# Attention in a fused attention and feed-forward layer on eight cores: the value matmuls six chunks behind the scores, and one eviction for two score chunks

## The reference

```python
q, k, v = xn @ Wq.T, xn @ Wk.T, xn @ Wv.T          # 16 heads of 128; 4 heads for k and v
q, k = rope(rms_norm(q)), rope(rms_norm(k))
bias = einsum('bhsr,bhtr->bhst', Rq, Rk)            # rank 32, heads 0..11
bias[:, :4] = (bias[:, :4] + transpose(bias[:, :4])) * 0.5   # heads 0..3 symmetric
scores = q @ k.T / sqrt(128) + bias * graph_scale   # heads 12..15: no bias
scores = where(causal, scores, min)
out = softmax(scores) @ v
s = out @ Wo.T
```

## Time and profile before

| | us |
|---|---|
| three runs, median | 4767.55 |
| lowest, highest | 4765.06, 4774.42 |
| the profiled execution's own time | 4769.61 |
| its span on core 1, the slowest | 4767.8 |
| spans of the eight cores | 4740.7 to 4767.8 |

### The profile page before, as it was taken

The page is one execution under the profiler, slowest core; times in us unless marked ns, Lnnn a source line. Parts: engine busy times, 40 slices in busy tenths (PEclk is TensorE's granted clock), DMA queues, the critical chain, the costliest instruction groups (busy, mean ns, idle before and its releaser), DMA issues. The chain is left out here.

```text
span 4767.8 us, 39041 instructions; the slowest of 8 cores (4740.7 to 4767.8 us)
## 1 busy us (share of the span) xinstructions
PE 3630.5 (76%) x15274; PEld 1513.7 (32%) x15274; DVE 1171.4 (25%) x1403; ACT 876.4 (18%) x862; POOL 315.5 (7%) x311
## 2 busy tenths in 40 slices
PE   2676576766999998988999998846666767775974
PEld 1222122222444443433444443311222222221433
DVE  7132133333000000000000000024444454453006
ACT  2121022221000000001000000013333343442112
POOL 0000000000111110001111100000000000000000
PEclk9977777777999999999999999967787888997986
DMA  3202411122788774557788754540000000003448
GB/s 133 53 9 22 106 29 27 29 31 31 73 78 77 74 71 71 75 75 79 74 78 78 74 66 77 76 117 21 18 18 16 16 7 15 15 6 84 39 98 279
DMA packets 547238, 287.88 MB, mean 60 GB/s; under 512 B 457075, under 2 KB 528756, under 8 KB 540020
## 3 DMA queue, kind: packets, MB, share of 16 engines
q0 software_dynamic: 498480, 162.55, 32.6%
q1 hardware_dynamic: 48580, 122.82, 7.6%
HBM read 397.53 MB, written 50.33 MB: 94 GB/s over the span
## 5 line engine op out<-in xcount | busy, mean ns | idle before, releaser
L856 PE MATMUL p_dps<-p_hfm,p_dwb 128*128 128x512 bf16 x2816 | 630.5, 387 | 87.5 <-ACT p_gout L874 59.0
L784 PE MATMUL p_gps<-xn_fm,p_gwb 128*128 128x512 bf16 x2816 | 627.0, 381 | 35.5 <-DMA p_uwb<-wu 35.4
L791 PE MATMUL p_ups<-xn_fm,p_uwb 128*128 128x512 bf16 x2816 | 622.1, 379 | 0.0
L1235 ACT ACTIVATE p_ptb<-p_scr,st_bnegb 128x1024 bf16<-128x1024 f32 x320 | 366.7, 1148 | 633.2 <-DVE p_scr L1202 448.4
L817 DVE SCALAR_TENSOR_TENSOR p_hfm<-p_ups,c_ups,p_sg 128x1024 bf16<-128x1024 f32 x88 | 112.9, 1283 | 1502.8 <-ACT p_sg L806 1502.8
L856 PEld LDWEIGHTS p_dps<-p_hfm,p_dwb 128*128 128x128 bf16 x2816 | 278.4, 99 | 439.6 <-issue 124.6
L1111 PE MATMUL p_sc<-p_qg,p_kfm 128*128 128x512 bf16 x640 | 281.6, 454 | 165.3 <-DVE p_ogs L1178 97.3
L784 PEld LDWEIGHTS p_gps<-xn_fm,p_gwb 128*128 128x128 bf16 x2816 | 276.2, 98 | 373.1 <-issue 45.9
L791 PEld LDWEIGHTS p_ups<-xn_fm,p_uwb 128*128 128x128 bf16 x2816 | 275.6, 98 | 332.2
L806 ACT ACTIVATE p_sg<-p_gps,c_gates 128x1024 f32<-128x1024 f32 x88 | 98.0, 1114 | 1090.9 <-PE p_ups L791 1090.8
L670 PE MATMUL p_qps<-xn_fm,p_wbuf 128*128 128x512 bf16 x1024 | 265.0, 424 | 39.3 <-DMA p_wbuf<-wq 39.3
(11 more groups left out here) (135 smaller groups left out, 2344.4 us busy)
## 6 DMA issues: line engine op xcount, KB each, us to landing
p_gwb<-wg POOLq DMA_DIRECT2D x88, 512.0 KB, 8.9
p_uwb<-wu POOLq DMA_DIRECT2D x88, 512.0 KB, 10.7
p_dwb<-wd POOLq DMA_DIRECT2D x88, 512.0 KB, 5.7
p_xt<-x SPq DMA_DIRECT2D x32, 1024.0 KB, 7.0
y<-p_outb SPq DMA_DIRECT2D x16, 1024.0 KB, 10.6
p_wbuf<-wq POOLq DMA_DIRECT2D x16, 512.0 KB, 6.5
sp_q<-p_qout SPq DMA_DIRECT2D x64, 128.0 KB, 1.8
sp_g<-p_gout SPq DMA_DIRECT2D x32, 256.0 KB, 2.6
```

The lines of the kernel that those rows point to most:

```text
L784: tensor.matmul(gps[:, po + q4 * 512:po + (q4 + 1) * 512], gw_[:, ec * 128:(ec + 1) * 128], xn_cols(ec, hh * 1024 + q4 * 512, 512), start= ...
L791: mm = tensor.matmul(ups[:, po + q4 * 512:po + (q4 + 1) * 512], uw_[:, ec * 128:(ec + 1) * 128], xn_cols(ec, hh * 1024 + q4 * 512, 512), s ...
L856: mm = tensor.matmul(dps[:, oc4 * 1024 + q4 * 512: oc4 * 1024 + (q4 + 1) * 512], wv_[:, oc4 * 128:(oc4 + 1) * 128], hfm[:, ic * 1024 + q4 ...
L1235: scalar.activation(ptb[:, j0 * 512:(j0 + 2) * 512], scr[:, (pr % 3) * 1024:(pr % 3) * 1024 + 1024], AF.Exp, bias=bneg_b[:, col:col + 1]). ...
```

## The change

TensorE's stream in attention has the value matmul of chunk j - 6 instead of j - 3 behind the scores of chunk j; six of them, not three, stand at the head's end. VectorE evicts a pair whose two chunks both are unmasked by one copy of 1024 columns, after a wait for both; pairs with a masked chunk are evicted as before, in two parts. Buffers, their number, the semaphores' counts and ScalarE's stream stay the same.

```diff
@@ -1129,15 +1129,15 @@
                                     last.then_inc(eC.h, 1)
                                     eC.inc()
                                     ich += 1
-                                    if j >= 3:
-                                        jj = j - 3
+                                    if j >= 6:
+                                        jj = j - 6
                                         tensor.wait_ge(eEx.h, base_eEx + pbase + jj // 2 + 1)
                                         tensor.matmul(
                                             o_ps[:, (h % 2) * 512:(h % 2) * 512 + 512],
                                             vsb[:, jj * 512 + kv * 128: jj * 512 + (kv + 1) * 128],
                                             ptb[:, jj * 512:(jj + 1) * 512],
                                             start=(jj == 0), stop=False)
-                                for jj in range(max(0, nch - 3), nch):
+                                for jj in range(max(0, nch - 6), nch):
                                     tensor.wait_ge(eEx.h, base_eEx + pbase + jj // 2 + 1)
                                     tensor.matmul(
                                         o_ps[:, (h % 2) * 512:(h % 2) * 512 + 512],
@@ -1186,25 +1186,36 @@
                             for h in range(NH):
                                 if h >= 1:
                                     sums_evac(vector, h - 1)
-                                for j in range(nch):
+                                for j in range(0, nch, 2):
                                     pr = ich // 2
-                                    if pr >= 3 and ich % 2 == 0:
+                                    if pr >= 3:
                                         vector.wait_ge(eEx.h, base_eEx + pr - 2)
-                                    vector.wait_ge(eC.h, base_eC + ich + 1)
-                                    po = (pr % 2) * 1024 + (ich % 2) * 512
-                                    so = (pr % 3) * 1024 + (ich % 2) * 512
-                                    if j >= 4 * g:
-                                        k = j - 4 * g
-                                        op = vector.tensor_tensor(
-                                            scr[:, so:so + 512], sc_ps[:, po:po + 512],
-                                            masks[:, k * 512:(k + 1) * 512], ALU.add)
-                                    else:
-                                        op = vector.tensor_copy(
-                                            scr[:, so:so + 512], sc_ps[:, po:po + 512])
-                                    if ich % 2 == 1:
-                                        op.then_inc(eEv.h, 1)
+                                    po = (pr % 2) * 1024
+                                    so = (pr % 3) * 1024
+                                    if j + 1 < 4 * g:
+                                        vector.wait_ge(eC.h, base_eC + ich + 2)
+                                        vector.tensor_copy(
+                                            scr[:, so:so + 1024], sc_ps[:, po:po + 1024]
+                                        ).then_inc(eEv.h, 1)
                                         eEv.inc()
-                                    ich += 1
+                                        ich += 2
+                                        continue
+                                    for jc in (j, j + 1):
+                                        vector.wait_ge(eC.h, base_eC + ich + 1)
+                                        poc = po + (ich % 2) * 512
+                                        soc = so + (ich % 2) * 512
+                                        if jc >= 4 * g:
+                                            k = jc - 4 * g
+                                            op = vector.tensor_tensor(
+                                                scr[:, soc:soc + 512], sc_ps[:, poc:poc + 512],
+                                                masks[:, k * 512:(k + 1) * 512], ALU.add)
+                                        else:
+                                            op = vector.tensor_copy(
+                                                scr[:, soc:soc + 512], sc_ps[:, poc:poc + 512])
+                                        if ich % 2 == 1:
+                                            op.then_inc(eEv.h, 1)
+                                            eEv.inc()
+                                        ich += 1
                                 if h >= 1:
                                     tail(vector, h - 1)
                             sums_evac(vector, NH - 1)
```

## The result

The changed kernel takes 4674.4 us in the median of its executions and the kernel before 4771.7. In some executions of either kernel the cores of one die run at a lower granted clock and the time is longer (5109 and 4819 us for two of the changed kernel's); these medians count them, the ratios here leave them out. The ratio is 0.9805 (0.9782 to 0.9827), 93 us. Run again on another occasion it had 0.9769 (0.9735 to 0.9802). The forecast was 78 us, 4690.

The account below looks back on a forecast made before the run. The prediction took attention to be bound by a circle through ScalarE's exponential. Savings of 14.9, 39.4 and 23.5 us gave 78, so 4767.55 - 78 = 4690; the forecast's own range was 4676 to 4704 (0.65), the overall range 4658 to 4722.

Parts of the forecast that it names:

- What bounds the kernel: Attention, g = 1 to 3: no engine full; a chain bounds it, with 126.0 us of TensorE idle awaiting exponentials at L1135.
- the old circle: Attention at lag three: exponential, value matmul, second chunk's scores, eviction, next-but-one exponential; 3.64 us per two pairs, heads 4 to 11.
- What is late next: Attention after the change, per pair: TensorE's slots 1.72 (heads 0-3), score buffers 1.41 (4-11) and 1.20 (12-15).
- the buffer circle: Two PSUM score buffers: scores of pair p+2 wait for pair p's eviction; 2.82 us per two pairs in heads 4-11.
- The rival of a larger gain: VectorE releases TensorE in 0.14, circles 1.355 and 1.14: 85 us, 99 with edges; range 4655 to 4676, chance 0.12.
- The edges: Head entries and ends: 0.37 to 0.53 us against, other effects for; 0.3 a head either way, 14 us, taken as nothing.
- Heads 4 to 11: Attention, two score matmuls a chunk: 1.82 to 1.41 us a pair, 0.41 saved, 39.4 us in all.
- Heads 0 to 3: Attention, three score matmuls a chunk: 2.03 to 1.72 us a pair, 0.31 saved, 14.9 us in all.
- Heads 12 to 15: Attention, one score matmul a chunk: 1.69 to 1.20 us a pair, 0.49 saved, 23.5 us in all.
- the second rival: Larger gain in attention through a quicker VectorE release, 4668; with a copy of 0.69, 12 us more, 4656; chance 0.12.
- the third rival: Attention slower if TensorE stays longer at 1.2 GHz: granted clock 0.75 costs 115 us, 4805; chance 0.03.
- The clock as a way to slower: Attention, g = 1 to 3: a mean granted clock of about 0.79 would eat the 78 us; chance 0.03.

Follow-up runs that it names:

- e1: Kernel before with the value matmul's lag raised from 3 to 6 and 512-wide copies kept (changed kernel without the wide copy): ratio 0.9717, attention 1010.2 us.
- e2: Kernel before with the wide copy alone, the lag staying at three: ratio 1.0102, attention 1193.0 us.
- e5: Lag six, narrow copies, and TensorE's wait at a head's start moved to before its first value matmul; against the kernel before: ratio 0.9629, attention 974.8 us.
- e8: Kernel before plus nine needless matmuls ahead of TensorE's wait at each head's start (heads 2 to 15): ratio 0.9938, attention 1111.4 us.
- e7: Changed kernel plus nine needless matmuls ahead of TensorE's wait at each head's start; against the kernel before: ratio 0.9731, attention 1016.8 us.

## Why the prediction was right, and where its sizes were off

- **What bounds the kernel** was right: the wait of L1135 for the exponential went, and with it 99 us of attention time in g = 1 to 3, nothing in g = 0. e1 shows that the lag does all of it, and e2 that the wide copy alone makes the old circle 0.54 longer.
- **What is late next** was right for heads 4 to 11: the two score buffers. The way back from VectorE to TensorE was the term that was mis-sized: 0.25 taken, 0.15 measured, the buffer circle 2.71 and not 2.82. Over 96 and 48 pairs at 0.055 it is 8 us. I had the choice between this value and the 0.14 of ScalarE's way, and took the row of the same pair of engines. That row was of the wait for a product at a head's start. TensorE had been idle for 2 us there, but that isn't the reason: in e5 33 waits for an eviction end more than 1.5 us of idle time, and the way is 0.15 in all of them. Why the product's way is longer stays open. The rival of a larger gain, with 1.355 a pair, describes what happened, and the time (4674) lies in its range, 2 us under the forecast's own.
- **The edges** were the other mis-sized term. The step that failed is "I allow 0.3 either way and take nothing". It is seen best between e8 and e7, where the fill holds the clock up in both kernels and the change gains 104 us in heads 0 to 15. By the forecast's own sum, with the shorter way back, the rates give 85: 15, 45 and 26 in heads 0 to 3, 4 to 11 and 12 to 15, against 24.8, 49.2 and 30.0 measured. The other 19 us are 0.39 a head. In heads 0 to 3 the excess over the rate is 3.1, 3.3 and 3.5 us in g = 1, 2 and 3, the same however many pairs a head has, so it does lie at the edges. ScalarE in a head of g = 3, number 0 to 3, of e8 and of e7:

```profile
4027.20 2.44 ACT L1242 ACTIVATE p_ptb<-p_scr,st_bnegb 128x1024 bf16<-128x1024 f32 x2 [8.35 <-DVE p_scr L1209]
4031.28 1.15 ACT L1242 ACTIVATE p_ptb<-p_scr,st_bnegb 128x1024 bf16<-128x1024 f32 x1 [1.63 <-DVE p_scr L1209]
...
3999.95 2.44 ACT L1253 ACTIVATE p_ptb<-p_scr,st_bnegb 128x1024 bf16<-128x1024 f32 x2 [8.89 <-DVE p_scr L1204]
4002.89 1.15 ACT L1253 ACTIVATE p_ptb<-p_scr,st_bnegb 128x1024 bf16<-128x1024 f32 x1 [0.49 <-DVE p_scr L1204]
```

From the first exponential to the third it is 4.08 us in e8 and 2.94 in e7. That is 1.14 less, where the rate gives 0.31. The other 0.83 a head, 3.3 us in four heads, is the old kernel's stand at the first exponential, which the forecast named among the edges and took as nothing.

- **Heads 4 to 11** of the pair itself: 39.4 us forecast, 37.4 measured on core 1 (470.7 to 433.3). This is partly luck of the core: by the medians of the eight cores it is 44. On core 1 a worse clock in g = 1 hides some of the gain: heads 4 to 7 had run at 1.00 before and have 0.91 now, and gained only 1 us where 3 were due.
- **Heads 0 to 3**: 14.9 forecast, 26.8 measured (263.1 to 236.3); 26.5 by the medians. It is the edges above, and no matter of the clock, since it is 24.8 with the fill.
- **Heads 12 to 15**: 23.5 forecast, 35.5 measured (230.1 to 194.6); 33 by the medians. A part of the excess is the clock's, and my sentence that the clock's part was in the 0.3 a head was wrong here: held up by the fill, the old kernel gives 15.5 us in these heads and the new one 10.0 (12.1 and 10.3 by the medians). The difference lies in g = 1 and 2, where the fill takes 5.5 and 4.7 us off the old kernel and 1.0 and 3.2 off the new one; in g = 3 it is 5.2 and 5.7. Why the new kernel loses less to the low clock in short heads isn't shown. With the clock held up in both the gain is 30.0, of which the shorter way back explains 2.6; the rest, some 4 us, is again at the edges.
- **The wide copy** was priced right in itself (1.223 us) and in the old circle (e2). Its cost in the changed kernel, 31 us of attention time, is larger than the 23 to 26 that the same walk through the heads gives; what stays of it, some 6 us, I can't assign. It goes with a granted clock of 0.84, 0.87 and 0.89 against e1's 0.85, 0.89 and 0.91, but no run separates the two.
- **Slips in the sums**, which moved nothing: in the second rival a copy of 0.69 takes the circle from 1.355 to 1.29, so it gives 6 us more and not 12, and the lowest time is 4662 and not 4656. Six slots of 0.262 are 1.57 and not 1.59. In the third rival the time at 1.2 GHz grows by 222 us and not 230, which costs 111: 4801.
- **The clock as a way to slower** didn't come: it is 0.84, 0.87 and 0.89 in the three stretches where it was 0.84, 0.88 and 0.90, far from the 0.79 at which it would have decided. The Trainium skill's rule of a die held to 13/16 (TensorE: Matmul & The Clock Gate, Part 1) is in part borne out by these runs, which the trace of the kernel before couldn't show. There no core is ever at this level. In the changed kernel's profile cores 0 and 1 are at 0.81 for 101 and 116 us in their first 0.4 ms (the row in the section on the result), and cores 2 and 3 for 169 us each behind their attention stage; cores 4 to 7 never are. But dense matmuls on all cores don't bring it by themselves: from 1200 to 1800 us of its span every core of both profiles is over 97% busy at 0.99 or 1.00. None of it falls into the attention stages that are compared here.

## What to carry to other kernels

A wait inside a loop is best read as a circle: list every step from one instruction to the same one a turn later, count how many items it carries, and compare that with each engine's own work per item. Then do the same for the edges of the loop, by walking one whole turn; rates alone missed a fifth of the gain here. Joining two evictions saves VectorE 0.06 us a pair and costs 0.4 to 0.5 us of delay wherever the next stage or the buffer waits for the first half, so it pays only where the pieces are ready together.

## What the runs showed of the hardware

- Needless matmuls in 2 us of idle time ahead of every head raised TensorE's granted clock from 0.69 to 0.91 in the sparsest heads and made the kernel 0.6% faster (0.4 to 0.9%).
- From the end of VectorE's eviction to the matmul that waits for it was 0.15 us in all 45 waits of the changed kernel, and also in the 33 waits of e5 that end more than 1.5 us of idle time. From the end of a head's product to the next matmul it was 0.25 to 0.26 in most of 39 waits, and up to 0.43. From the end of an exponential to the value matmul it was 0.14 (166 waits of the kernel before).
- 512-wide fp32 copies out of PSUM start 0.60 apart in a row, and 1024-wide ones 1.13: the width saves 0.06 a pair.
- With the same dense matmuls on all eight cores the granted clock of cores 0 to 3, one die, was 0.81 for 101 to 169 us of one profiled execution of the changed kernel, in e7's that of cores 4 to 7 for 150 to 219 us, and in eleven of the fourteen profiles it never was.
